# Folding a down-projection weight by two split products on data prepared by GpSimd, in place of one fp32 product a tile

## What is computed

```python
x = fwht(x * SU_ug) / SCALE
x_up = x @ W_up.T * (Wscale_ug[:INTER] * SCALE)
x_gate = x @ W_gate.T * (Wscale_ug[INTER:] * SCALE)
x = jax.nn.silu(x_gate) * x_up
x = fwht(x * SU_dp) / SCALE
x = x @ W_down.T * (Wscale_dp * SCALE)
```

## Time and profile before

| what | value |
|---|---|
| median of 3 runs | 2015.33 us (2013.12 to 2015.95) |
| the profiled execution | 2014.63 us |
| its span, first to last instruction | 2012.9 us |
| mean granted TensorE clock | 0.990 |
| TensorE matmul busy | 1939.8 us |
| VectorE busy | 1374.8 us |
| ScalarE busy | 860.6 us |
| GpSimd busy | 196.7 us |

### The profile page before, as it was taken

One profiled execution on the slowest core, in us unless ns is written; L12 is line 12 of the kernel. 1 busy time (PEld: TensorE's weight loads), 2 busy tenths in 40 slices (PEclk: granted clock), 3 DMA queues, 4 the chain that ended last, 5 costly groups with the idle time before them and its releaser, 6 DMA issues.

```text
span 2012.9 us, 31356 instructions
## 1 busy us (share of the span) xinstructions
PE 1939.8 (96%) x10848; PEld 1512.0 (75%) x10848; DVE 1374.8 (68%) x3302; ACT 860.6 (43%) x1615; POOL 196.7 (10%) x554
## 2 busy tenths in 40 slices
PE   6899999999999999899999999999999999999998
PEld 3566666666666556546888788999999999999997
DVE  6777776677767555676555887677676777767755
ACT  3366555556556554465222443332333323333221
POOL 3111111111111111012000000010010100101000
PEclk8899999999999999999999999999999999999999
DMA  7443344334433455553535988789788797887884
GB/s 234 124 106 76 100 111 112 97 85 108 112 97 77 138 168 165 153 194 116 211 130 194 368 322 337 288 298 340 282 298 331 297 336 291 298 337 286 319 312 165
DMA packets 115738, 423.28 MB, mean 210 GB/s; under 512 B 28015, under 2 KB 33391, under 8 KB 101373
## 3 DMA queue, kind: packets, MB, share of 16 engines
q1 hardware_dynamic: 103916, 370.87, 55.0%
q10 hardware_dynamic: 11664, 50.40, 6.7%
HBM read 317.12 MB, written 61.10 MB: 188 GB/s over the span
## 4 chain that ended last, share of the span: by engine, by line
PE 45%; DVE 5%; ACT 2%; DMA 1%; issue 1%; SPq 0%; POOL 0%; DVEq 0%; ACTq 0%
PE banks L1773 22%; PE banks L1864 15%; PE banks L1642 7%; DVE ln_stats L1196 1%; PE banks L1739 1%; PE banks L1733 1%; DMA upgate_items_dram<-items_ring 1%; DVE x_normed L1208 0%; DVE y L1321 0%; ACT silu_gate L880 0%; DMA upgate_raw<-in_w_ug 0%; ACT y_split L865 0%; ACT L880 0%; ACT L886 0%; DVE out_sb L1393 0%
## 5 line engine op out<-in xcount | busy, mean ns | idle before, releaser
L1864 PE MATMUL banks<-d_ring,y_split 128*128 128x512 f32 x1536 | 377.5, 392 | 1.9 <-DVE y_split L1341 1.9
L973 ACT ACTIVATE probs<-banks 128x512 f32<-128x512 f32 x576 | 312.5, 600 | 59.7 <-PE banks L1910 54.1
L1864 PEld LDWEIGHTS banks<-d_ring,y_split 128*128 128x128 f32 x1536 | 281.7, 188 | 56.8 <-DVE y_split L1341 2.1
L1773 PE MATMUL banks<-h_t_split,items_ring 128*128 128x256 f32 x2280 | 321.0, 283 | 1.9 <-DVE both L1298 1.9
L1773 PEld LDWEIGHTS banks<-h_t_split,items_ring 128*128 128x128 f32 x2280 | 298.9, 191 | 13.7 <-ACT h_t L791 4.0
L1933 PE MATMUL banks<-probs,v_ones 128*64 128x512 f32 (+3 forms) x1536 | 280.4, 500 | 3.1 <-POOL probs L1065 3.1
L1696 PE MATMUL banks<-k_stack,q_stacks 96*128 96x512 f32 (+3 forms) x768 | 252.0, 372 | 16.3 <-ACT neg_max_rows L742 5.7
L1910 PE MATMUL banks<-q_stacks,k_stack 98*128 98x512 f32 (+3 forms) x768 | 251.1, 369 | 6.0 <-ACT probs L973 4.3
L1933 PEld LDWEIGHTS banks<-probs,v_ones 128*64 128x64 f32 x1536 | 118.9, 138 | 164.2 <-issue 136.5
L1773 PE MATMUL banks<-input_sums,items_ring 128*128 128x256 f32 x1710 | 236.2, 283 | 0.0
L1065 POOL TENSOR_SCALAR_AFFINE_SELECT probs<-probs 128x128 f32<-128x128 f32 x512 | 147.9, 313 | 746.8 <-ACT probs L973 746.8
(11 more groups left out here) (185 smaller groups left out, 2240.5 us busy)
## 6 DMA issues: line engine op xcount, KB each, us to landing
items_ring<-upgate_items_dram SPq DMA_DIRECT2D x94, 1792.0 KB, 7.3
d_ring<-down_split_dram SPq DMA_DIRECT2D x128, 512.0 KB, 8.0
q_stacks<-q_split SPq DMA_DIRECT2D x192, 128.0 KB, 2.5
o_group<-o_raw SPq DMA_DIRECT2D x128, 128.0 KB, 2.3
upgate_raw<-in_w_ug SPq DMA_DIRECT2D x32, 512.0 KB, 4.7
upgate_items_dram<-items_ring ACTq DMA_DIRECT2D x8, 1792.0 KB, 7.4
upgate_items_dram<-items_made ACTq DMA_DIRECT2D x8, 1792.0 KB, 6.7
x<-in_x SPq DMA_DIRECT2D x32, 256.0 KB, 3.1
```

Source lines behind the costliest of these rows:

```text
L973: nc.scalar.activation(pr[:, u, :], score_bank[:, at % SLOTS_SCORE, :], ACT.Exp, scale=SCALE).then_inc(exped, 1)
L1773: last = nc.tensor.matmul(item_bank(g, item), weights[:, a, item, k * P:(k + 1) * P], by_key(item_input(blk, item, m))[:, k, :], start=(k ...
L1864: last = nc.tensor.matmul(acc[:, t, :], ys[s][:, a, t * P:(t + 1) * P], dr[g % D_RING][:, m, :], start=(f == 0 and a + m == 0), stop=(f == ...
```

## The change

Each folding tile is now split by GpSimd (`split_fold`): it copies the loaded tile into an fp32r tile, waits for that, and subtracts to get the rest. TensorE waits for the split and makes two fp32r products that add up in one bank. There is a single pair of parts, so a split first waits until the fold product before it is done. GpSimd's program now walks all units; the split of the tile of unit 4 stands behind the triangles of unit 2, in general `SPLIT_BEFORE = 2` units ahead of its product. The matrix `across` is loaded raw and copied to fp32r by GpSimd once. The buffers move (the parts take a place that `h2_t` uses later), and the turns move: the first from head 60 unit 6 to head 61 unit 2, the last now at head 61 unit 8.

```diff
-FOLD_RING = 4
+FOLD_RING, SPLIT_BEFORE = 4, 2
 BLOCK_IN, STAT_LEFT, NORM_LEFT, CROSS_LEFT, CAST_LEFT = 7, 6, 5, 2, 1
-TURNS, HADS = [(4, 6), (3, 2), (3, 4), (3, 6)], [(1, 1), (1, 3), (1, 5), (1, 7)]
+TURNS, HADS = [(3, 2), (3, 4), (3, 6), (3, 8)], [(1, 1), (1, 3), (1, 5), (1, 7)]
...
-            place(s, "under_across", [P, 2 * KT * P])
-            W["across"] = place(s, "across", [P, P])
+            W["parts"] = place(s, "fold_parts", [P, 2, D], F32R)
+            W["across_raw"], W["across"] = place(s, "across_raw", [P, P]), place(s, "across", [P, P], F32R)
...
-                        act.dma_start(across[:], io["across"]).then_inc(across_in, 16)
+                        act.dma_start(across_raw[:], io["across"]).then_inc(across_in, 16)
...
+            def split_fold(kind, i):
+                use = (FT if kind == "along" else 0) + i
+                if use == 0:
+                    pool.wait_ge(across_in, 16)
+                    nc.gpsimd.tensor_copy(across[:], across_raw[:])
+                pool.wait_ge((raw_in if kind == "across" else again_in)[i % FOLD_RING], 16 * (i // FOLD_RING + 1))
+                if use:
+                    side_filled(pool, (kind, i - 1) if i else ("across", FT - 1))
+                tile = (raw if kind == "across" else again)[:, i % FOLD_RING, :]
+                nc.gpsimd.tensor_copy(fold_parts[:, 0, :], tile).then_inc(fold_taken, 1)
+                pool.wait_ge(fold_taken, use + 1)
+                nc.gpsimd.tensor_tensor(fold_parts[:, 1, :], tile, fold_parts[:, 0, :].bitcast(F32), ALU.subtract).then_inc(fold_ready, 1)
+
             for H in range(ALL):
...
+                for u in range(NU):
+                    if u in TRIANGLES:
+                        clear_triangles(H, u)
+                    for kind in ("across", "along"):
+                        for i, (_, left, at) in enumerate(f for f in FOLDS if f[0] == kind):
+                            if (left, at) == (ALL - H, u + SPLIT_BEFORE):
+                                split_fold(kind, i)
...
                 kind, i = key
...
-                    last = nc.tensor.matmul(side[:, r, :], across[:], raw[:, i % FOLD_RING, :], start=True, stop=True)
...
-                    last = nc.tensor.matmul(side[:, r, :], had[:].bitcast(F32), again[:, i % FOLD_RING, :], start=True, stop=True)
+                pe.wait_ge(fold_ready, (FT if kind == "along" else 0) + i + 1)
+                r = side_slot(key)
+                for a in range(2):
+                    last = nc.tensor.matmul(side[:, r, :], (across if kind == "across" else had)[:], fold_parts[:, a, :], start=a == 0, stop=a == 1)
                 last.then_inc(side_full[r], 1)
```

More of the change, by code:

```diff
@@ L347, in phase @@
     x1, xr = x1xr[:, 0:2, :], x1xr[:, 2:4, :]
-    raw, fold, again, across = W["raw"], W["fold"], W["again"], W["across"]
+    raw, fold, again, across_raw, across, fold_parts = (W[n] for n in ("raw", "fold", "again", "across_raw", "across", "parts"))
     fx1, xn, hs, hb, fht = F["x1"], F["xn"], F["hs"], F["hb"], F["ht"]
@@ L393, in phase @@
     across_in, raw_in, again_in = sem("across_in"), [sem(f"raw_in{n}") for n in range(FOLD_RING)], [sem(f"again_in{n}") for n in range(FOLD_RING)]
+    fold_taken, fold_ready = sem("fold_taken"), sem("fold_ready")
     fold_hi, fold_out = sem("fold_hi"), [sem(f"fold_out{n}") for n in range(2)]
@@ L1058, in _, with clear_triangles @@
                 nc.gpsimd.tensor_tensor(q_split[:, 1, k, :], q_raw[:, k, :], q_split[:, 0, k, :].bitcast(F32), ALU.subtract).then_inc(qw_split_ready, 1)
-            for H in range(ALL):
[L1061 to L1067, removed]
+            def clear_triangles(H, u):
+                pool.wait_ge(exped, H * NU + u + 1)
+                for at in TRIANGLES[u]:
+                    triangle = pr[:, u, at:at + P]
+                    last = nc.gpsimd.affine_select(out=triangle, in_=triangle, compare_op=ALU.is_ge, fill=0.0, base=0,
+                                                   pattern=[[1, P]], channel_multiplier=-1)
+                last.then_inc(masked, 1)
+            def split_fold(kind, i):
[10 more added lines that the diff above has]
+                nc.gpsimd.tensor_tensor(fold_parts[:, 1, :], tile, fold_parts[:, 0, :].bitcast(F32), ALU.subtract).then_inc(fold_ready, 1)
+            for H in range(ALL):
+                for u in range(NU):
[5 more added lines that the diff above has]
+                                split_fold(kind, i)
             def sum_inputs(m):
@@ L1718, in fold_tile @@
                 kind, i = key
[L1719 to L1722, removed]
-                    last = nc.tensor.matmul(side[:, r, :], across[:], raw[:, i % FOLD_RING, :], start=True, stop=True)
-                else:
-                    pe.wait_ge(again_in[i % FOLD_RING], 16 * (i // FOLD_RING + 1))
-                    r = side_slot(key)
-                    last = nc.tensor.matmul(side[:, r, :], had[:].bitcast(F32), again[:, i % FOLD_RING, :], start=True, stop=True)
+                pe.wait_ge(fold_ready, (FT if kind == "along" else 0) + i + 1)
+                r = side_slot(key)
+                for a in range(2):
+                    last = nc.tensor.matmul(side[:, r, :], (across if kind == "across" else had)[:], fold_parts[:, a, :], start=a == 0, stop=a == 1)
                 last.then_inc(side_full[r], 1)
```

## The result

The changed kernel takes 2034.34 us (median of 6 runs, 2032.91 to 2041.24), the kernel before 2015.64 (6 runs): +18.7 us, ratio 1.0104, 95% interval 1.0094 to 1.0114. The profiled execution took 2034.43 us, its span is 2032.7. It is slower, as forecast, by 18.7 us where 10.9 were worked out.

What follows compares the result with a forecast made beforehand. TensorE, its matmuls busy for 96% of the span, was taken to bound the kernel. Saving -14.7, waits +20.5 and clock +5.1 gave +10.9 on 2014.63, plus 0.70: 2026.2 us, range 2014 to 2044.

Steps and rivals of the forecast that it cites:

- Where the split starts: Unit 4's split, behind unit 2's triangles, starts 0.17 us before TensorE arrives: 1.87 us wait; none at unit 8 in two-fold heads.
- Price of the split: On GpSimd: copy 0.62 us, subtraction 1.29; the chain from last triangle to first product 2.04 us, free as work.
- The rival of the slow copy: GpSimd's copy runs like the scaling, 2.07 us; longer waits and clock falls in all nine: +43, 2058 us; chance 0.10.
- Sum of the waits: TensorE's waits for splits over the folding heads, with the copy of `across`: 20.5 us.
- The nine at unit 4: Tiles of unit 4 in heads 46, 47, 48, 50, 51, 52, 58, 59, 60: 1.87 us wait each, 16.8 us.
- The saving: On TensorE, two fp32r products for one fp32: a tile from 0.98 to 0.52 us, 32 tiles, -14.7 us.
- the lower end given: Saving on TensorE's fold products if switching between kinds of product costs twice as much: -12.8 us.
- The clock: TensorE's granted clock falls to 1.2 GHz after some waits, 1.7 us a fall: +5.1 us, ends 0 to 15.3.
- I count three falls in the nine: Three of the nine unit-4 waits of 1.87 us lower TensorE's clock, 1.7 us each: +5.1 us.
- The Trainium skill's rule: Only longer gaps re-throttle TensorE; by it the clock term is 0 and the time 5.1 us less.
- Absorption: Rival: the fourteen heads' 15.4 us idle time absorbs the waits: -9.6, 2006 us; chance faster 0.12, partly, within 0.2%, 0.07.
- Blocking between GpSimd and VectorE: Rival: five GpSimd subtractions meet two-input VectorE operations in heads 49, 54, 57, 59: +5.5, 2032 us; chance 0.08.

Runs made afterwards that it cites:

- the wait alone: Changed kernel, with TensorE still waiting for GpSimd's split but making the one fp32 product of the raw tile as before; parts unused: 2049.07 us, ratio 1.0157.
- five units ahead: Changed kernel with each split placed five units ahead of its product instead of two: 2008.32 us, ratio 0.9954; run again 2008.39 us, 0.9959.
- the filled waits: Changed kernel with seven idle TensorE products of 512 columns put into each of ten waits for the split: 2027.79 us, ratio 1.0060.
- the splits alone: Kernel before plus all 32 GpSimd splits, five units ahead; TensorE doesn't wait and keeps its fp32 product, parts unused: 2015.88 us, ratio 1.0005.
- four units ahead: Changed kernel with each split placed four units ahead of its product instead of two: 2015.71 us, ratio 1.0002.

## Why the prediction was right, and where its sizes were off

- **Where the split starts.** Right. The list's "two units" were 0.17 us; the wait was put at 1.87 us and measures 1.80 in head 50 and, by the length of a head, 1.88. Unit 8 in two-fold heads doesn't wait.
- **Price of the split.** Right: copy 0.61 (0.62 taken), subtraction 1.26 (1.29). The rival of the slow copy fell with the first row.
- **Sum of the waits.** 20.5 forecast, 20.8 in the row of waits, and that they agree is partly luck. The nine at unit 4 read 14.8 us (17.1 forecast) and the other five 6.0 (3.4). Head 54 waited 1.93 us and not 0.75, for another reason than named: the load of its first tile (GpSimd itself waited 1.8 us for that transfer). In heads 49 and 57 unit 8 read 1.3 and 1.0, where 0.87 and a share of 0.3 were counted. With the tails that the rows leave out the sum is between 22 and 23 us.
- **The saving: mis-sized.** 0.385 us a tile and not 0.46, 12.3 us and not 14.7, just under the lower end given (12.8). At unit 8 a fold and its switch to the weighing take 0.63 us (1.03 before), where 0.46 + 0.06 were counted: 0.06 was read off an fp32 product with the fp32 weighing behind it, and behind a short product 0.15 to 0.17 are left over. That this is the switch wasn't isolated. The 14.7 us between the wait alone and the changed kernel are the forecast's number, but hold clock as well as products, so they don't confirm it.
- **The clock: mis-sized, and the larger part of the gap.** The step "I count three falls in the nine", +5.1 us, failed. Of the +18.9 us of heads 46 to 60, +18.8 are idle time and -12.3 the products; 12.4 are left, of which some 2 are the tails of the waits. So about 10 us, twice the term, go to the clock; it is what is left over, not a measurement of its own. By the granted clock six of the nine have the low level: 48, 50, 51 and 58 newly, and 46 and 59, which had a low stretch before, for twice as long. Two more are in heads 49 and 57, which the count left out, and there five units ahead shows a low stretch without a wait for a split in front. Heads 47, 52, 54 and 60 had waits as long and kept the clock; why these and not the others stays open (nor does the length decide: in five units ahead head 54 waited 2.5 us and kept it). The price of one, 1.7 us, was right (1.6).
- **The Trainium skill's rule** that gaps as short as these don't re-throttle (TensorE: Matmul & The Clock Gate, "HAM oscillation — how this bites in real kernels") would have made the term zero. The changed kernel and the filled waits both disagree.
- **Rivals.** Absorption: small. The waits for splits are 20.8 us and the idle time grew by 18.8; the folds' waits for VectorE shrank from 7.0 to 5.2 us. Blocking between GpSimd and VectorE: none in the changed kernel (VectorE is busy 141.27 us over these heads for 141.23), 4.5 us with the splits alone, and free of charge there.
- As measured, with the clock as the rest: 18.8 - 12.3 + 12.4 = 18.9; the forecast's terms were 20.5 - 14.7 + 5.1 = 10.9. The direction came from the right mechanism, and the clock's part lies between the ends given for it (none to nine falls, 0 to 15.3 us).

## What to carry to other kernels

A lead counted in units of a program isn't a lead in time: read off the trace when the instruction ahead of the new work ends and when its reader comes. Here three more units of lead, a change of one number and one condition, made 1.0104 into 0.9954. And a wait of 1 to 2 us on a saturated TensorE cost more than its length here: with the clock, the waits alone (21.4 us by the rows, some 23 with their tails) cost 33. In four units ahead, waits of 0.42 to 0.44 us in heads 47, 48, 50, 51, 52, 58 and 60 brought no low stretch. Count a wait of 1 to 2 us at about half again, or give the engine products to do while it waits. And look at the clock again after making a product shorter, not only after adding a wait.

## What the runs showed that was not expected

Filling waits with useless products was worth 6.5 us. A low stretch in heads 49 and 57 came with the shorter products even where no split was waited for.

An operation of VectorE with one small input in SBUF can be held as long as one with two large ones. In head 50 of five units ahead, the negation of eight maxima meets GpSimd's subtraction (VectorE, then GpSimd, in order of time):

```profile
739.34 1.28 DVE L1134 TENSOR_SCALAR neg_max<-max_all 128x8 fp32r<-128x8 f32 x1 [0.20 <-DVE max_all L1122]
```

```profile
739.32 1.27 POOL L1080 TENSOR_TENSOR fold_parts<-fold_raw,fold_parts 128x512 fp32r<-128x512 f32 x1
```

It takes 1.28 us; in the kernel before all 64 took 170 to 178 ns. It ends with GpSimd's operation (740.62 and 740.59), so it seems to have been held for the whole of it. Over heads 46 to 60 this line's 15 operations take 11.9 us for 2.6 before, which is 9.3 of the 9.5 us that VectorE is busier in five units ahead. The prediction had looked for two-input operations only. No engine's wait is put down to it in the profile, so no cost in time shows.
